# Attention states per head, in two float16 halves spread over 96 partitions, in place of a float32 product of four heads

## The chip, the cores and the metric

One Trainium2 chip, one core. The metric is the device time of one execution in microseconds (us). The work is spread over TensorE (PE, with its weight loads PEld), VectorE (DVE), ScalarE (ACT), GpSimd (POOL) and SyncE (SP), whose instruction stream issues nearly all DMAs into one hardware queue. Each engine runs its own instructions strictly in order.

## What is computed

Eight batches of 512 rows by 512 pass through a feed-forward block, an attention block and a second feed-forward block, each added to its input. The part that the change touches is the attention: 16 heads of 32, a row of 512 tokens in four chunks of 128, and a state S of 32x32 per head carried from chunk to chunk:

```python
def step(S, qkv_c):
    qi, ki, vi = qkv_c
    scores = jnp.einsum('bhtd,bhsd,hts->bhts', qi, ki, mask)
    intra = jnp.einsum('bhts,bhsd->bhtd', scores, vi)
    cross = jnp.einsum('bhtd,ht,bhde->bhte', qi, lam_t, S)
    o = scale * (intra + cross)
    kv = jnp.einsum('bhtd,ht,bhte->bhde', ki, lam_rev, vi)
    return (lam_T * S + kv, o)
```

lam_t is exp(-s t) for token t of a chunk, lam_rev exp(-s (128 - t)), lam_T exp(-128 s). A feed-forward block is silu(x W1) * (x W3), a Hadamard transform folded into W2, and a product with it.

## The kernel before

**Passes and slots.** There are 16 feed-forward passes (two per batch, in the list ORDER). A pass has 16 steps j; step j is `gate` (12 matmuls of 512 columns into g_bank), `lin` (12 into l_bank) and `down` of step j-1 (12 into the four d_banks). After each of the three lies a *slot*: pieces of the norms and of the attention are put there by hand, in `attention_slots`, so that PE has them between two blocks of 12. The attention of batch b starts at slot 1+78b; it has four groups of four heads, 12 slots apart, 32 groups in all. Every engine walks the same list STEPS and issues what it has of each step, so this list sets the order on every engine. The slots of a group, counted from its own slot `at`, are: q and k at -6 to -3, `kturn` (decayed keys, kdec) at -2, the first score at 0, and then what the diff shows.

**The last steps of a pass.** At step 0 of a pass comes `down` of the pass before, then `resid` 0 and 1 (DVE reads d_bank, L1146); `resid` 2 and 3 follow the gate of step 1. After `resid` 3 the queue of SP has the store of the 1 MB result (x_dram, L596, or out_dram, L593), and, when the pass was a first feed-forward, the load of the next input (xin, 1 MB, L599). `down` of step 0 waits for all four `resid`.

**A group.** `score` c is four matmuls (keys ks, queries qs, both spread over 96 partitions as three blocks of 32: high, high and low halves of float16 numbers) into a_bank 0. DVE multiplies by the mask (L1304), ACT rounds to float16 (L940), DVE takes the rest (L1309), and `pv` c uses both halves. `kv` makes three products kdec x values of 128x128 in a_bank 1, of which the 32x32 blocks on the diagonal are the heads' own; DVE multiplies by a block mask, diag (L1314). `state` makes two steps S = lam_T S + kv on 128x128 (L1326). `pv` c adds in a_bank 1, for chunks after the first, the float32 product of qdec and state (L1514) and per head two float16 products (L1519 with 64 columns, L1521 with 32). Two chunks share the bank, and one DVE reduction (L1332) takes both. qdec is the queries times lam_t, made on POOL (L715).

**Spreading.** q and k are stored to parts_dram and loaded again as three blocks each (L644, L650), since a DMA alone moves data between partitions here.

Of the kernel before, what the change touches and what calls it, by code (L numbers as in the profile page):

```python
# [7 lines left out]
ALU = mybir.AluOpType  # L8
# [16 lines left out]
SCORE_SCALE = 2.0 ** -20  # L25


def macaron_kernel(nc, x, qkv_w, qkv_norm_w, proj_w, proj_norm_w, norm_w, s, w1, w2, w3, out):
# [24 lines left out]
    with ctx:  # L53
# [3 lines left out]
        def sem(name):  # L57
# [21 lines left out]
        sizes = dict(x1=TT * D, hid=2 * D, gate=D, hfull=D, x2=TT * D, yt=KT * T, qs=HG * T // 2, ks=HG * T // 2, qdec=T,  # L79
                     kdec=(TT - 1) * P, flow=T, sc=2 * HG * P, state=(TT - 1) * P)  # L80
# [11 lines left out]
        gate, hfull, qdec, flow = at["gate"], at["hfull"], at["qdec"], at["flow"]  # L92
# [31 lines left out]
        state = at["state"].rearrange("p (c e) -> p c e", c=TT - 1)  # L124
        first = sizes["x1"] + sizes["hid"] + sizes["gate"] + sizes["hfull"]
# [28 lines left out]
        lam_rev = sb("lam_rev", [P, HEADS])  # L154
        lam_T = sb("lam_T", [P, GROUPS])
        diag = sb("diag", [P, P])
# [52 lines left out]
        q_hi, q_lo, q_dec = sem("q_hi"), sem("q_lo"), sem("q_dec")  # L209
# [10 lines left out]
        state_done = sem("state_done")  # L220
# [61 lines left out]
        def attention_slots():  # L282
# [11 lines left out]
            for b in range(B):  # L294
# [5 lines left out]
                for g in range(GROUPS):  # L300
# [118 lines left out]
        def bank_use(step, arg):  # L419
            if step in ("turn", "v"):  # L420
                return arg[1] % 2, 2
            if step == "proj":
                return arg[1] % 2, 1
            if step == "pv":
                return (1, 1) if arg[2] % 2 == 0 else None
            return {"q": (0, 1), "k": (0, 1), "score": (0, 1), "kv": (1, 1)}.get(step)
# [4 lines left out]
        for step, arg in STEPS:  # L431
# [6 lines left out]
            elif step == "pv":  # L438
                USES[step, arg] = USES["pv", arg[:2] + (arg[2] - 1,)]
# [44 lines left out]
        def _(sp):  # L484
# [34 lines left out]
            for step, arg in STEPS:  # L519
# [109 lines left out]
                elif step == "klow":  # L629
# [8 lines left out]
                    if ag:  # L638

                        b, fill = filled("score", ((ag - 1) // GROUPS, (ag - 1) % GROUPS, TT - 1))  # L640
                        sp.wait_ge(a_ready[b], fill)
# [4 lines left out]
                elif step == "kspread":  # L646
                    ag = arg[0] * GROUPS + arg[1]
                    sp.wait_ge(k_stored, 16 * (ag + 1))
                    for i, part in enumerate((0, 0, 1)):
                        sp.dma_start(ks[HD * i:HD * (i + 1)],  # L650
                                     parts_dram[ag % 2, 1, :, part].rearrange("(h p) t -> p h t", h=HG)).then_inc(k_moved, 16)
                elif step == "split":
# [26 lines left out]
        def _(pool):  # L679
# [17 lines left out]
            for step, arg in STEPS:  # L697
# [8 lines left out]
                elif step == "q":  # L706
                    b, g = arg
                    if g:

                        bank_pv, fill = filled("pv", (b, g - 1, TT - 1))  # L710
                        pool.wait_ge(a_ready[bank_pv], fill)

                    bank_q, _ = filled(step, arg)
                    pool.wait_ge(a_free[bank_q], copied(step, arg, bank_q) + 1)
                    nc.gpsimd.tensor_tensor(qdec.rearrange("p (c t) -> p c t", c=TT), qT[:].rearrange("p (c t) -> p c t", c=TT),  # L715
                                            lam_t[:, g:g + 1, :].to_broadcast([P, TT, P]), ALU.mult).then_inc(q_dec, 1)
# [29 lines left out]
                elif step == "decay":  # L746
# [6 lines left out]
                    nc.gpsimd.iota(junk[:, P:2 * P], [[1, P]], base=0, channel_multiplier=0,  # L753
# [9 lines left out]
        def _(act):  # L763
# [14 lines left out]
            for step, arg in STEPS:  # L778
# [43 lines left out]
                elif step == "decay":  # L822
# [7 lines left out]
                    for g in range(GROUPS):  # L830
                        nc.scalar.activation(lam_t[:, g, :], junk[:, P:2 * P], ACT.Exp, scale=s_col[:, g:g + 1])

                    nc.scalar.activation(decay_bound[:], decay_bound[:], ACT.Exp, scale=float(P)).then_inc(decay_top, 1)
                    nc.scalar.activation(lam_rev[:], s_row[:], ACT.Exp, scale=tiny[:, 0:1])
# [57 lines left out]
                elif step == "q":  # L892
# [3 lines left out]
                    if ag:  # L896

                        act.wait_ge(q_lo, ag)
                        act.wait_ge(q_dec, ag)
# [31 lines left out]
                elif step == "kturn":  # L931

                    act.wait_ge(kd_f32, arg[0] * GROUPS + arg[1] + 1)
                    nc.scalar.copy(kdec[:, 0, :], kT[:, 0:(TT - 1) * P]).then_inc(kd_hi, 1)
                elif step == "score":
# [7 lines left out]
        def _(dve):  # L943
# [34 lines left out]

            link(nc.vector.memset(diag[:], 0.0))
            for h in range(HG):  # L980
                nc.vector.memset(diag[HD * h:HD * (h + 1), HD * h:HD * (h + 1)], SCORE_SCALE)

            for step, arg in STEPS:
# [88 lines left out]
                elif step == "fit":  # L1072
# [6 lines left out]
                    nc.vector.tensor_scalar(lam_rev[:], lam_rev[:], decay_bound[:], None, ALU.mult)  # L1079
# [110 lines left out]
                elif step == "ostat":  # L1190
                    a, t = arg

                    b, _ = filled("pv", (a, GROUPS - 1, 2))
                    dve.wait_ge(a_free[b], copied("pv", (a, GROUPS - 1, 2), b) + 1)
# [86 lines left out]
                elif step == "kturn":  # L1281
# [5 lines left out]
                    for c in range(TT - 1):  # L1287
                        decayed = kT[:, P * c:P * (c + 1)].rearrange("p (h d) -> p h d", h=HG)
                        ins = nc.vector.tensor_tensor(decayed, decayed, lam_rev[:, HG * arg[1]:HG * (arg[1] + 1)].rearrange("p (h a) -> p h a", a=1)
# [20 lines left out]
                elif step == "kv":  # L1310
# [17 lines left out]
                elif step == "pv" and arg[2] % 2:  # L1328
# [3 lines left out]
                    nc.vector.tensor_reduce(x2[:, c - 1:c + 1, P * g:P * (g + 1)],  # L1332
# [223 lines left out]
```

## Time and profile before

| | |
|---|---|
| median of 3 runs | 2354.49 us (2353.8 to 2356.52) |
| the profiled execution | 2355.63 us, span 2353.9 us |
| PE busy | 2336.4 us (99%) |
| DVE / ACT / POOL busy | 1232.0 / 692.4 / 149.8 us |
| mean granted PE clock | 0.999 of full speed |
| moved by DMA | 196.83 MB, 84 GB/s |

The span is the stretch between the first and the last instruction in the trace; the own time of the profiled execution has 1.73 us more around it. A busy share counts an engine as busy while any of its instructions is in flight; matmuls overlap, so the start times of PE's pieces say more than their durations.

### The profile page before, as it was taken

The page shows a single profiled execution, that of the slowest core. Times are in us where ns is not written, and L with a number is a line of the kernel's source. Part 1 is how long each engine was busy: PE and PEld are TensorE (multiplying, and loading weights), DVE is VectorE, ACT ScalarE, POOL GpSimd, SP SyncE. Part 2 cuts the span into 40 slices and gives each one's busy share as a digit, 9 for nine tenths or more (in the row PEclk, how much of TensorE's full clock was granted, in tenths as well). Part 3 has the DMA queues.
Part 4 walks back from the last instruction along what each step waited for, and adds up shares of the span by engine and source line. Part 5 has one row for each costly group of instructions (what it writes and reads, how often), then busy time and mean ns, then how long its engine had stood idle before and what let it go on. Part 6 is the DMA issues. An engine that isn't in the chain of part 4 may idle for free.

```text
span 2353.9 us, 31017 instructions
## 1 busy us (share of the span) xinstructions
PE 2336.4 (99%) x12407; PEld 1120.7 (48%) x12407; DVE 1232.0 (52%) x2211; ACT 692.4 (29%) x1164; POOL 149.8 (6%) x126
## 2 busy tenths in 40 slices
PE   8999999999999999999999999999999999999999
PEld 4444444444544454445444444445444544544444
DVE  6577555654565446546554465544664455445212
ACT  6645233222222222223223222222232213221211
POOL 0190000000000000000000000000000000000000
PEclk9999999999999999999999999999999999999999
DMA  8856622331243212422042223421432224131200
GB/s 218 229 152 175 157 86 64 89 86 50 68 77 107 72 28 82 103 75 64 28 138 51 54 81 90 99 54 28 121 68 85 50 54 99 31 87 36 65 25 19
DMA packets 299457, 196.83 MB, mean 84 GB/s; under 512 B 231600, under 2 KB 256176, under 8 KB 295472
## 3 DMA queue, kind: packets, MB, share of 16 engines
q1 hardware_dynamic: 299024, 194.31, 31.6%
q8 instruction: 98, 1.61, 0.3%
q10 hardware_dynamic: 288, 0.52, 0.1%
q14 instruction: 47, 0.39, 0.1%
HBM read 84.68 MB, written 54.53 MB: 59 GB/s over the span
## 4 chain that ended last, share of the span: by engine, by line
PE 94%; DVE 3%; issue 1%; ACT 1%; DMA 1%; SPq 0%; POOL 0%; DVEq 0%; ACTq 0%; POOLq 0%
PE d_bank L1437 27%; PE l_bank L1417 27%; PE g_bank L1417 26%; PE a_bank L1472 5%; PE a_bank L1532 2%; PE a_bank L1455 2%; PE a_bank L1483 1%; PE a_bank L1514 1%; PE a_bank L1519 1%; PE a_bank L1497 1%; DVE work L1146 1%; DVE work L1126 0%; DMA w1t<-kT 0%; PE a_bank L1521 0%; PE d_bank L1391 0%
## 5 line engine op out<-in xcount | busy, mean ns | idle before, releaser
L1437 PE MATMUL d_bank<-w2t,work 128*128 128x512 f16 x2940 | 671.9, 379 | 0.0
L1437 PEld LDWEIGHTS d_bank<-w2t,work 128*128 128x128 f16 x2940 | 284.7, 98 | 332.4 <-DVE work L1146 0.6
L1126 DVE SCALAR_TENSOR_TENSOR work<-l_bank,l_scale,work 128x512 f32<-128x512 f32 x256 | 191.8, 749 | 468.4 <-PE l_bank L1417 468.4
L1417 PE MATMUL g_bank<-xt,w1t 128*128 128x512 f16 x1536 | 354.1, 380 | 3.6 <-DMA w1t<-kT 3.6
L1417 PE MATMUL l_bank<-xt,w3t 128*128 128x512 f16 x1536 | 352.4, 379 | 0.0
L857 ACT ACTIVATE work<-g_bank,g_scale 128x512 f32<-128x512 f32 x256 | 175.4, 685 | 490.1 <-PE g_bank L1417 488.2
L876 ACT CAST work<-work 128x512 f16<-128x512 f32 x232 | 143.3, 618 | 562.0 <-DVE work L1126 561.1
L1417 PE MATMUL l_bank<-work,w3t 128*128 128x512 f16 x1344 | 308.4, 379 | 0.2 <-DVE work L1126 0.2
L1417 PE MATMUL g_bank<-work,w1t 128*128 128x512 f16 x1344 | 308.3, 379 | 0.0
L1417 PEld LDWEIGHTS g_bank<-xt,w1t 128*128 128x128 f16 x1536 | 148.3, 98 | 177.9 <-DMA w1t<-kT 4.6
L1417 PEld LDWEIGHTS l_bank<-xt,w3t 128*128 128x128 f16 x1536 | 148.1, 98 | 173.0 <-issue 0.2
L1417 PEld LDWEIGHTS l_bank<-work,w3t 128*128 128x128 f16 x1344 | 129.6, 98 | 152.6 <-DVE work L1126 0.7
L1417 PEld LDWEIGHTS g_bank<-work,w1t 128*128 128x128 f16 x1344 | 129.7, 98 | 152.1
L1133 DVE TENSOR_TENSOR work<-work 128x512 f16<-128x512 f32 x232 | 160.3, 691 | 60.2 <-ACT work L876 59.5
L1309 DVE TENSOR_TENSOR work<-work 128x512 f16<-128x512 f32 x128 | 88.6, 692 | 88.1 <-ACT work L940 88.1
L884 ACT CAST cent<-cent 128x512 f16<-128x512 f32 x124 | 76.5, 617 | 173.8 <-DVE cent L1240 60.3
L1472 PE MATMUL a_bank<-zt,wqkv 128*128 128x512 f16 x512 | 121.0, 379 | 0.0
L940 ACT CAST work<-work 128x512 f16<-128x512 f32 x128 | 79.0, 618 | 126.8 <-DVE work L1304 126.8
L715 POOL TENSOR_TENSOR work<-qT,lam_t 128x512 f32<-128x512 f32 x32 | 40.7, 1271 | 1071.8 <-ACT qT L900 1071.8
L1260 DVE TENSOR_TENSOR cent<-cent 128x512 f16<-128x512 f32 x124 | 85.3, 688 | 35.1 <-ACT cent L884 32.8
L705 POOL TENSOR_TENSOR rstd<-veps,half 128x4 f32<-128x4 f32 x32 | 37.0, 1156 | 891.6 <-DVE veps L1188 546.9
L1304 DVE SCALAR_TENSOR_TENSOR work<-a_bank,mask 128x512 f32<-128x512 f32 x128 | 87.3, 682 | 2.1
(227 smaller groups left out, 1791.1 us busy)
## 6 DMA issues: line engine op xcount, KB each, us to landing
work<-parts_dram SPq DMA_DIRECT2D x192, 128.0 KB, 2.7
x_dram<-work SPq DMA_DIRECT2D x16, 1024.0 KB, 4.2
work<-x_dram SPq DMA_DIRECT2D x11, 1024.0 KB, 6.6
parts_dram<-q_parts SPq DMA_DIRECT2D x32, 256.0 KB, 2.0
parts_dram<-k_parts SPq DMA_DIRECT2D x32, 256.0 KB, 2.2
norm_dram<-cent SPq DMA_DIRECT2D x32, 256.0 KB, 2.0
w2t<-in_L_ffn_W_dram SPq DMA_DIRECT2D x30, 256.0 KB, 3.2
xin<-in_L_attn_x_dram SPq DMA_DIRECT2D x7, 1024.0 KB, 8.4
```

Of the source, the lines that this page charges most:

```text
L857: nc.scalar.activation(gate, g_bank[:], ACT.Silu, scale=g_scale[:, j:j + 1]).then_inc(gate_ready, 1)
L876: nc.scalar.copy(parts[:, 0, :], hfull).then_inc(hi_ready, 1)
L884: nc.scalar.copy(halves[:, t % 2, 0, :], centred).then_inc(ln_hi, 1)
L940: nc.scalar.copy(sc[:, c % 2, 0], flow.rearrange("p (h t) -> p h t", h=HG)).then_inc(sc_hi, 1)
L1126: nc.vector.scalar_tensor_tensor(out=hfull, in0=l_bank[:], scalar=l_scale[:, j:j + 1], in1=gate, op0=ALU.mult, op1=ALU.mult).then_inc(hful ...
L1133: nc.vector.tensor_tensor(parts[:, 1, :], hfull, parts[:, 0, :], ALU.subtract).then_inc(lo_ready, 1)
L1260: nc.vector.tensor_tensor(halves[:, t % 2, 1, :], centred, halves[:, t % 2, 0, :], ALU.subtract).then_inc(ln_lo, 1)
L1304: nc.vector.scalar_tensor_tensor(out=masked, in0=a_bank[b][:].rearrange("p (h t) -> p h t", h=HG), scalar=SCORE_SCALE, in1=mask[:, HG * g: ...
L1309: nc.vector.tensor_tensor(sc[:, c % 2, 1], masked, sc[:, c % 2, 0], ALU.subtract).then_inc(sc_lo, 1)
L1417: ins = nc.tensor.matmul(dst[:], wt[:, wp, k, P * j:P * (j + 1)], src[:, xp, k, :], start=(k == 0 and wp == xp), stop=(k == KT - 1 and wp ...
L1437: ins = nc.tensor.matmul(d_bank[t][:], parts[:, hp, P * t:P * (t + 1)], w2t[:, j, wp, :], start=(j == 0 and hp == wp), stop=(j == HT - 1 a ...
L1472: ins = nc.tensor.matmul(a_bank[b][:], wqkv[:, k, col:col + P], zt[:, part, k, :], start=(k == 0 and part == 0), stop=(k == KT - 1 and par ...
```

## The change

The states are kept per head as 32 columns instead of 128 (DVE copies the diagonal blocks of `kv`, four instructions of 32 partitions), rounded into two float16 halves by ACT and DVE, stored to state_dram, and loaded as three blocks of 32 partitions into `states` (high, high, low). `pv` multiplies per head the *undecayed* queries qs (high, low, high) of the scores with them, on 96 partitions and 32 columns, into a region of its own of a_bank 1, and DVE multiplies this region by the decay lam_out when it takes the result, then adds the two others. Each chunk now takes a_bank 1 for itself. qdec and its POOL product are gone, as are lam_t and diag. Scales that are powers of two (lift, lower) keep the halves in range. `kv` and `state` come one slot earlier, `pv` 1 to 3 one slot later.

```diff
-                    add(slots, at, [("score", (b, g, 0))])
-                    add(slots, at + 1, [("kv", (b, g)), ("score", (b, g, 1)), ("state", (b, g))])
-                    for c in range(TT):
-                        add(slots, at + 2 + c, [("pv", (b, g, c))] + ([("score", (b, g, c + 2))] if c < TT - 2 else []))
+                    add(slots, at, [("kv", (b, g)), ("state", (b, g)), ("score", (b, g, 0))])
+                    add(slots, at + 1, [("score", (b, g, 1)), ("statestore", (b, g))])
+                    add(slots, at + 2, [("pv", (b, g, 0)), ("score", (b, g, 2)), ("statespread", (b, g))])
+                    add(slots, at + 4, [("pv", (b, g, 1)), ("score", (b, g, 3))])
+                    add(slots, at + 5, [("pv", (b, g, 2))])
+                    add(slots, at + 6, [("pv", (b, g, 3))])
...
+                elif step == "statestore":
+                    ag = arg[0] * GROUPS + arg[1]
+                    sp.wait_ge(state_lo, ag + 1)
+                    if ag >= 2:
+
+                        sp.wait_ge(state_moved, 16 * BLOCKS * (ag - 1))
+                    sp.dma_start(state_dram[ag % 2], state_parts).then_inc(state_stored, 16)
+                elif step == "statespread":
+                    ag = arg[0] * GROUPS + arg[1]
+                    sp.wait_ge(state_stored, 16 * (ag + 1))
...
+                    for i, part in enumerate((0, 0, 1)):
+                        sp.dma_start(states[HD * i:HD * (i + 1)],
+                                     state_dram[ag % 2, :, part].rearrange("(h p) c e -> p h c e", h=HG)).then_inc(state_moved, 16)
...
-                    nc.gpsimd.tensor_tensor(qdec.rearrange("p (c t) -> p c t", c=TT), qT[:].rearrange("p (c t) -> p c t", c=TT),
-                                            lam_t[:, g:g + 1, :].to_broadcast([P, TT, P]), ALU.mult).then_inc(q_dec, 1)
...
+                elif step == "state":
+                    ag = arg[0] * GROUPS + arg[1]
+                    act.wait_ge(state_done, (TT - 2) * (ag + 1))
...
+                    nc.scalar.copy(state_parts[:, 0], state).then_inc(state_hi, 1)
...
-            link(nc.vector.memset(diag[:], 0.0))
-            for h in range(HG):
-                nc.vector.memset(diag[HD * h:HD * (h + 1), HD * h:HD * (h + 1)], SCORE_SCALE)
...
+                    nc.vector.tensor_scalar(lam_out[:, 0], lam_out[:, 0], SCORE_SCALE / STATE_SCALE, None, ALU.mult)
+
+                    nc.vector.tensor_scalar(lower_col[:], lam_T[:], 1.0, None, ALU.max)
+                    link(nc.vector.tensor_scalar(lift[:], lift[:], 1.0, None, ALU.max))
...
+                    link(power(lower[:], lift[:], True))
...
+                    for c in range(1, TT - 1):
+                        nc.vector.tensor_tensor(lam_rev[:, c], lam_rev[:, c - 1], lower[:], ALU.mult)
+                        link(nc.vector.tensor_tensor(lam_out[:, c], lam_out[:, c - 1], lift[:], ALU.mult))
...
-                    nc.vector.tensor_tensor(state, a_bank[b][:, 0:(TT - 1) * P].rearrange("p (c e) -> p c e", c=TT - 1),
-                                            diag[:].rearrange("p (a e) -> p a e", a=1).to_broadcast([P, TT - 1, P]),
-                                            ALU.mult).then_inc(a_free[b], 1)
+                    products = a_bank[b][:, 0:(TT - 1) * P].rearrange("p (c h e) -> p c h e", c=TT - 1, h=HG)
+                    for h in range(HG):
+
+                        rows_h = slice(HD * h, HD * (h + 1))
+                        ins = nc.vector.tensor_scalar(state[rows_h], products[rows_h, :, h], STATE_SCALE, None, ALU.mult)
+                    ins.then_inc(a_free[b], 1)
...
+                    dve.wait_ge(state_hi, ag + 1)
+                    nc.vector.tensor_tensor(state_parts[:, 1], state, state_parts[:, 0], ALU.subtract).then_inc(state_lo, 1)
...
+                        nc.vector.tensor_tensor(o.rearrange("p (h e) -> p h e", h=HG), turns[:, 0].rearrange("p (h e) -> p h e", h=HG),
+                                                lam_out[:, c - 1, HG * g:HG * (g + 1)].rearrange("p (h a) -> p h a", a=1)
+                                                .to_broadcast([P, HG, HD]), ALU.mult).then_inc(o_sum, 1)
+                        dve.wait_ge(o_sum, done + 1)
+                        nc.vector.tensor_tensor(o, turns[:, 1], o, ALU.add).then_inc(o_sum, 1)
+                        dve.wait_ge(o_sum, done + 2)
+                        nc.vector.tensor_tensor(o, turns[:, 2], o, ALU.add).then_inc(a_free[b], 1)
...
+                    if c == 1:
+                        pe.wait_ge(state_moved, 16 * BLOCKS * (a * GROUPS + (g + 1)))
...
-                        nc.tensor.matmul(halves_o[:, 0, :], qdec[:, P * c:P * (c + 1)], state[:, c - 1, :],
-                                         start=(c == 2), stop=False, skip_group_check=True)
...
+                            ins = nc.tensor.matmul(turns[:, 0, cols], qs[0:BLOCKS * HD, h, P * c:P * (c + 1)],
+                                                   states[0:BLOCKS * HD, h, c - 1, :], start=False, stop=True, skip_group_check=True)
```

SP's queue in group 3 of batch 2, which starts with step 0 of a pass. Before the change (L644 and L650 load the queries and keys, L596 stores the result of the pass that ends, L599 loads the next input, L663 is the next norm):

```order
L644 DMA work<-parts_dram 32x4x512 x3
L650 DMA work<-parts_dram 32x4x512 x3
L596 DMA x_dram<-work 128x2048
L599 DMA xin<-in_L_attn_x_dram 128x4x512
L663 DMA_TRANSPOSE zt<-cent 128x8x128
```

and with the change, at the same place (L604 and L607 are the store and the load, L666 stores the states, L675 spreads them):

```order
L652 DMA work<-parts_dram 32x4x512 x3
L658 DMA work<-parts_dram 32x4x512 x3
L666 DMA state_dram<-work 128x192
L604 DMA x_dram<-work 128x2048
L607 DMA xin<-in_L_attn_x_dram 128x4x512
L675 DMA work<-state_dram 32x4x96 x3
L688 DMA_TRANSPOSE zt<-cent 128x8x128
```

The two transfers of 1 MB now stand between the store of the states and their spreading. They stand so in groups 0 of batch 0, 3 of batch 2 and 2 of batch 4; in group 1 of batch 6 it is the 1 MB store of an output alone.

DVE in the same group, before (L1126 is `lin`, L1304 and L1309 a score, L1133 `low`, L1146 `resid`, L1314 `kv`, L1326 `state`):

```order
L1126 SCALAR_TENSOR_TENSOR work<-l_bank,l_scale,work 128x512
L1304 SCALAR_TENSOR_TENSOR work<-a_bank,mask 128x512
L1309 TENSOR_TENSOR work<-work 128x512
L1133 TENSOR_TENSOR work<-work 128x512
L1146 SCALAR_TENSOR_TENSOR work<-d_bank,ffn_unscale,xin 128x512 x2
L1314 TENSOR_TENSOR work<-a_bank,diag 128x384
L1304 SCALAR_TENSOR_TENSOR work<-a_bank,mask 128x512
L1309 TENSOR_TENSOR work<-work 128x512
L1326 SCALAR_TENSOR_TENSOR work<-work,lam_T 128x128 x2
L1146 SCALAR_TENSOR_TENSOR work<-d_bank,ffn_unscale,xin 128x512 x2
```

and with the change (L1156, L1334, L1339, L1163, L1176 are the same steps under new line numbers; L1348 copies the diagonal blocks, L1359 is the recurrence, L1363 the low halves):

```order
L1156 SCALAR_TENSOR_TENSOR work<-l_bank,l_scale,work 128x512
L1348 TENSOR_SCALAR work<-a_bank 32x96 x4
L1359 SCALAR_TENSOR_TENSOR work<-work,lam_T 128x32 x2
L1363 TENSOR_TENSOR work<-work 128x96
L1334 SCALAR_TENSOR_TENSOR work<-a_bank,mask 128x512
L1339 TENSOR_TENSOR work<-work 128x512
L1163 TENSOR_TENSOR work<-work 128x512
L1176 SCALAR_TENSOR_TENSOR work<-d_bank,ffn_unscale,xin 128x512 x2
L1334 SCALAR_TENSOR_TENSOR work<-a_bank,mask 128x512
L1339 TENSOR_TENSOR work<-work 128x512
L1176 SCALAR_TENSOR_TENSOR work<-d_bank,ffn_unscale,xin 128x512 x2
```

All the work on the states now stands ahead of the first score and of the four `resid`.

## Rows read from the trace of the kernel before

**Rows 1.** The page's chain that ended last: share of the span by engine.

```profile
PE 94%; DVE 3%; issue 1%; ACT 1%; DMA 1%; SPq 0%; POOL 0%; DVEq 0%; ACTq 0%; POOLq 0%
```

**Rows 2.** Timeline of PE, one `pv` and a score: start us, us, engine, line.

```profile
556.46 0.38 PE L1514 MATMUL a_bank<-work 128*128 128x128 f32 x2
556.68 0.19 PE L1519 MATMUL a_bank<-work 128*128 128x64 f16 x1
...
556.90 0.38 PE L1483 MATMUL a_bank<-work 96*128 96x128 f16 x4
```

**Rows 3.** Groups by line and shape: busy us, mean ns, idle before.

```profile
L994 DVE TENSOR_SCALAR k_turned_parts<-k_turned_parts 128x4 f32<-128x4 f32 x7 | 1.2, 170 | 0.2
L934 ACT CAST work<-kT 128x384 f16<-128x384 f32 x32 | 16.3, 511 | 58.2 <-DVE kT L1289 58.2
```

**Rows 4.** Timeline of DVE in an ordinary group (group 0 of batch 2).

```profile
545.47 0.56 DVE L1294 TENSOR_TENSOR work<-kT,work 128x384 f16<-128x384 f32 x1 [0.58 <-ACT work L934]
547.49 0.75 DVE L1126 SCALAR_TENSOR_TENSOR work<-l_bank,l_scale,work 128x512 f32<-128x512 f32 x1 [1.46 <-PE l_bank L1417]
...
553.26 0.73 DVE L1326 SCALAR_TENSOR_TENSOR work<-work,lam_T 128x128 f32<-128x128 f32 x2
```

**Rows 5.** DMA issues of the page: KB each, median us to landing.

```profile
work<-parts_dram SPq DMA_DIRECT2D x192, 128.0 KB, 2.7
parts_dram<-q_parts SPq DMA_DIRECT2D x32, 256.0 KB, 2.0
xin<-in_L_attn_x_dram SPq DMA_DIRECT2D x7, 1024.0 KB, 8.4
zt<-cent SPq DMA_TRANSPOSE x68, 3.4
```

**Rows 6.** Timeline of DVE in group 3 of batch 2: second score, `resid` 2 and 3.

```profile
906.34 0.68 DVE L1304 SCALAR_TENSOR_TENSOR work<-a_bank,mask 128x512 f32<-128x512 f32 x1
...
908.96 1.40 DVE L1146 SCALAR_TENSOR_TENSOR work<-d_bank,ffn_unscale,xin 128x512 f32<-128x512 f32 x2
```

**Rows 7.** Timeline of PE in the same group.

```profile
901.12 0.39 PE L1483 MATMUL a_bank<-work 96*128 96x128 f16 x4
901.34 2.75 PE L1437 MATMUL d_bank<-w2t,work 128*128 128x512 f16 x12
903.93 0.67 PE L1497 MATMUL a_bank<-work 128*128 128x128 f16 x9
904.44 0.39 PE L1483 MATMUL a_bank<-work 96*128 96x128 f16 x4
...
911.02 0.40 PE L1483 MATMUL a_bank<-work 96*128 96x128 f16 x4
```

**Rows 8.** Timeline of SP's issues in the same group.

```profile
910.39 0.34 SPq L596 DMA_DIRECT2D x_dram<-work  x1
910.78 0.43 SPq L599 DMA_DIRECT2D xin<-in_L_attn_x_dram  x1
```

**Rows 9.** DMA issues of 460.6 to 461.8 us: KB each, us to landing.

```profile
xin<-in_L_attn_x_dram SPq DMA_DIRECT2D x1, 1024.0 KB, 8.3
zt<-cent SPq DMA_TRANSPOSE x1, 8.9
```

**Rows 10.** A stretch: length, busy PE, PEld, DVE, ACT, POOL, granted clock, DMA, GB/s.

```profile
38.00:40.00 2.00, 2.00 (x6) 0.76 (x5) 0.16 (x1) 0.00 (x0) 0.00 (x0) 0.50 1.22 287
```

**Rows 11.** Timeline of PE: a block of 12 after a wait, and a score after one.

```profile
36.02 4.45 PE L1417 MATMUL g_bank<-xt,w1t 128*128 128x512 f16 x12 [2.83 <-DMA w1t<-kT]
...
308.50 0.40 PE L1483 MATMUL a_bank<-work 96*128 96x128 f16 x4 [0.75 <-DVE work L1304]
```

**Rows 12.** Timeline of DVE: the block mask at the start, and the four `resid` of pass 0.

```profile
5.42 0.47 DVE L981 MEMSET diag<- 32x32 f32 x4
...
248.93 2.72 DVE L1146 SCALAR_TENSOR_TENSOR work<-d_bank,ffn_unscale,xin 128x512 f32<-128x512 f32 x4
```

**Rows 13.** The chain in order of time: start us, us, what (`down` of passes 0 and 1).

```profile
208.60 72.52 PE d_bank L1437 x336
```

More of the change, by code:

```diff
@@ L25 @@
 SCORE_SCALE = 2.0 ** -20
+STATE_SCALE = 2.0 ** -23
 def macaron_kernel(nc, x, qkv_w, qkv_norm_w, proj_w, proj_norm_w, norm_w, s, w1, w2, w3, out):
@@ L77, in macaron_kernel @@
         junk = qT
-        sizes = dict(x1=TT * D, hid=2 * D, gate=D, hfull=D, x2=TT * D, yt=KT * T, qs=HG * T // 2, ks=HG * T // 2, qdec=T,
-                     kdec=(TT - 1) * P, flow=T, sc=2 * HG * P, state=(TT - 1) * P)
+        sizes = dict(x1=TT * D, hid=2 * D, gate=D, hfull=D, x2=TT * D, yt=KT * T, qs=HG * T // 2, ks=HG * T // 2,
+                     kdec=(TT - 1) * P, flow=T, sc=2 * HG * P, state=(TT - 1) * HD, state_parts=(TT - 1) * HD,
+                     states=HG * (TT - 1) * HD // 2)
         early_use = sizes["x1"] + sizes["hid"] + sizes["gate"] + sizes["hfull"] + KT * H + 2 * T
@@ L124, in macaron_kernel @@
         state = at["state"].rearrange("p (c e) -> p c e", c=TT - 1)
+        state_parts = at["state_parts"].bitcast(F16).rearrange("p (a c e) -> p a c e", a=2, c=TT - 1)
+        states = at["states"].bitcast(F16).rearrange("p (h c e) -> p h c e", h=HG, c=TT - 1)
+        state_dram = nc.dram_tensor("state_dram", [2, P, 2, TT - 1, HD], F16, kind="Internal").ap()
         first = sizes["x1"] + sizes["hid"] + sizes["gate"] + sizes["hfull"]
@@ L424, in bank_use @@
             if step == "pv":
-                return (1, 1) if arg[2] % 2 == 0 else None
+                return 1, 1
             return {"q": (0, 1), "k": (0, 1), "score": (0, 1), "kv": (1, 1)}.get(step)
@@ L638, in _ @@
                     if ag:
-                        b, fill = filled("score", ((ag - 1) // GROUPS, (ag - 1) % GROUPS, TT - 1))
+                        b, fill = filled("pv", ((ag - 1) // GROUPS, (ag - 1) % GROUPS, TT - 1))
                         sp.wait_ge(a_ready[b], fill)
@@ L829, in _ @@
                     ins.then_inc(decay_exp, 1)
-                    for g in range(GROUPS):
-                        nc.scalar.activation(lam_t[:, g, :], junk[:, P:2 * P], ACT.Exp, scale=s_col[:, g:g + 1])
                     nc.scalar.activation(decay_bound[:], decay_bound[:], ACT.Exp, scale=float(P)).then_inc(decay_top, 1)
-                    nc.scalar.activation(lam_rev[:], s_row[:], ACT.Exp, scale=tiny[:, 0:1])
+                    nc.scalar.activation(lam_rev[:, 0], s_row[:], ACT.Exp, scale=tiny[:, 0:1])
+                    nc.scalar.activation(lam_out[:, 0], s_row[:], ACT.Exp, scale=tiny[:, 11:12])
+                    nc.scalar.activation(lift[:], s_row[:], ACT.Exp, scale=float(P))
                     nc.scalar.activation(lam_T[:], s_col[:], ACT.Exp, scale=float(P)).then_inc(act_const, 1)
@@ L1327, in _ @@
                                                        in1=state[:, c, :], op0=ALU.mult, op1=ALU.add).then_inc(state_done, 1)
-                elif step == "pv" and arg[2] % 2:
+                    dve.wait_ge(state_hi, ag + 1)
+                    nc.vector.tensor_tensor(state_parts[:, 1], state, state_parts[:, 0], ALU.subtract).then_inc(state_lo, 1)
+                elif step == "pv":
                     a, g, c = arg
@@ L1331, in _ @@
                     dve.wait_ge(a_ready[b], fill)
-                    nc.vector.tensor_reduce(x2[:, c - 1:c + 1, P * g:P * (g + 1)],
-                                            a_bank[b][:].rearrange("p (c a e) -> p c e a", c=2, a=2), AX.X, ALU.add
-                                            ).then_inc(a_free[b], 1)
+                    turns = a_bank[b][:].rearrange("p (r e) -> p r e", r=4)
+                    o = x2[:, c, P * g:P * (g + 1)]
+                    if c == 0:
+                        nc.vector.tensor_reduce(o, turns[:, 1:3].rearrange("p a e -> p e a"), AX.X, ALU.add).then_inc(a_free[b], 1)
+                    else:
+                        done = 2 * ((a * GROUPS + g) * (TT - 1) + c - 1)
+                        nc.vector.tensor_tensor(o.rearrange("p (h e) -> p h e", h=HG), turns[:, 0].rearrange("p (h e) -> p h e", h=HG),
[5 more added lines that the diff above has]
+                        nc.vector.tensor_tensor(o, turns[:, 2], o, ALU.add).then_inc(a_free[b], 1)
                 elif step == "proj":
```

66 lines of the change are left out of this document (32 added, 34 removed).

## The prediction

> **What bounds the kernel now.** I read the page's chain first: 94% of the span is PE, 1% DMA [rows 1], so a microsecond taken from PE is a microsecond of the result, and so is every wait put before PE. Then PE's timeline through one group, for what each small product really costs; then DVE and SP through an ordinary group and through a group that meets the end of a pass, for what reaches PE late. POOL's product, which the change removes, ends nothing on this chain.
>
> **PE's own work.** Durations overlap; start times count. The float32 product begins at 556.46 and the next matmul at 556.68: 0.22 us. The eight small ones take 556.68 to 556.90, 27.5 ns each, the 32-column ones no less than the 64-column ones [rows 2]. The new cross product is four of 32 columns, 4 x 27.5 ns = 0.11 us. Gain 0.11 us per chunk, for the 3 chunks of each of 32 groups that have a cross term, 96 in all: **-10.6 us**. Bounds: if a 32-column matmul next to another took half, -15.5; if each took 55 ns, as the four 128-column scores take, 0. I take the row of its own shape.
>
> The Trainium skill (TensorE: Matmul & The Clock Gate, Wait — 56ns, not 53.3ns?) says that start-to-start never falls below about 25 ns however few the columns. The trace's 27.5 ns agrees; by the page's figure the gain would be 11.5 us.
>
> **An ordinary group.** Times from the score at 547.29, which now gives its place to `kv`. Its keys kdec end at 546.03 [rows 4], so the earlier `kv` finds them. `kv` takes 0.5, 903.93 to 904.44 [rows 7]. DVE is free of `lin` at 548.2 [rows 4]. Then come four copies of 32x96: a DVE operation of 4 columns takes 0.17, one step on 128 columns 0.73/2 = 0.36 [rows 3, 4]; I take 0.18 each, 0.7; two state steps on 32 columns at 0.25, 0.5; ACT's rounding 0.3 (384 columns take 0.51 [rows 3]); the low half 0.2. The halves are ready at about 549.9. The store lands in 2.0, the three loads are issued 0.46 apart (one issue takes 0.43 [rows 8]) and each lands in 2.7 [rows 5]: about 555.6. PE asks for them in `pv` 1, behind four blocks of 2.59 (901.34 to 903.93 [rows 7]), `kv`, two scores, `pv` 0 and a third: 559.0. They are hidden with 3.4 us over. DVE's longer `pv` (three operations of 128 columns in place of half a reduction, 0.9 us) has a block of 2.59 before the bank is wanted. So the ordinary groups, 28 of 32, cost nothing. If the margin were gone, each us of lateness would cost 28.
>
> **The four groups at the end of a pass.** In group 3 of batch 2 the state work, 0.7 + 0.5 + 0.3 + 0.2 = 1.7, now stands before the first score; of it 0.46 stood there already for `kv` and 0.65 for the steps before `resid` 2. Three things follow.
>
> First, the second score leaves its bank 1.7 - 0.46 = 1.2 later than 906.34 + 0.61, at 908.2; PE, with nothing else late, wants it at 907.46: a wait of 0.8. Now the group has 0.3, before the fourth score (904.44 + 0.22 + 2 x 2.59 + 2 x 0.44 = 910.72, begun at 911.02 [rows 7]), which the longer wait replaces. **+0.5** in three such groups and in group 3 of batch 4, where a norm loads DVE in the same way: +2.0. In group 0 of batch 0 the second score follows the first at once; it waits 0.75 already [rows 11], and 1.2 of the 1.7 reaches it: +1.2.
>
> Second, and larger, SP. `resid` 3 ends at 910.36 [rows 6]; SP issues the store at 910.39 and the load of xin at 910.78 [rows 8]. Here `resid` 3 moves by 1.7 - 0.46 - 0.65 = 0.6, the load to 911.4, and only behind it can SP issue the spreading, 911.85 to 912.8. A transfer issued behind such a load lands with it: the transpose issued at 460.72, 0.5 after an xin load that took 8.3, took 8.9 itself [rows 9] where the median is 3.4 [rows 5]. So the states land about 0.6 after xin: 911.4 + 8.4 (median [rows 5]) + 0.6 = 920.4. PE arrives at `pv` 1 at 901.12 + 0.72 (kv, score) + 2.59 + 0.22 + 2.59 + 0.22 + 0.8 (wait) + 0.22 + 2 x 2.59 = 913.65. Wait: **+6.7**, in three groups: +20.2. In group 1 of batch 6 only the store of an output stands ahead: issued 911.85 to 912.8 by the same count and 2.7 to land, 915.5, 1.9 late without any queue; with the store 2.2.
>
> Third, the clock. After a wait of 2.83 us PE's granted clock falls from its full level, 2.4 GHz, to 0.50, 1.2 GHz [rows 10], and a block of 12 takes 4.45 instead of 2.75 [rows 11]: 1.7 lost. A wait of 7 us should do the same: 3 x 1.7 = **+5.1**, 0 if it doesn't, up to twice that if the low level lasts longer.
>
> The Trainium skill (DMA: Bandwidth & Descriptors, Queues, rings and completion order) says that on each DMA engine descriptors are consumed in ring order, all DMAs issued from SP sharing one ring on each. It speaks against this change; the trace agrees (8.9 beside 3.4). By that rule alone, with the load's 8.4 and nothing after it, the three waits would be 6.1 each, 1.8 less in all.
>
> **Constants and start.** `fit` gains 13 small DVE operations before the four `resid` of pass 0. Five are waited for, 0.17 each; the rest take between 0.08 pipelined and 0.17 [rows 3]: 1.5 to 2.2, taken 1.65. `resid` starts at 248.93 [rows 12], then 250.6, first one done at 251.25. PE's 192 matmuls of pass 0 end at 208.60 + 192 x 0.2155 = 249.95 [rows 13]: +1.3. The block mask of DVE's start goes (0.47 and its clearing, 0.7 in all) [rows 12]; the first weights' transfers hide most of it, since PE waits for one at 36.02 [rows 11]: -0.3, between 0 and -0.7.
>
> **Sum.** -10.6 + 2.0 + 1.2 + 20.2 + 2.2 + 5.1 + 1.3 - 0.3 = +21.1. Against the profiled execution, 2355.63, that is 2376.7; it stands 1.1 above the median of the runs shown, so 2375.6 on that.
>
> **Rivals.**
> (a) *The spreading isn't held by the transfers ahead of it.* It lands 2.7 after its last issue, 915.5 in place of 920.4, with no clock lost: four waits of 1.9. -10.6 + 2.0 + 1.2 + 7.6 + 1.3 - 0.3 = +1.2, 2355.7. For it: the transfer is small, 24 KB a load. Against: rows 9. Chance 0.12.
> (b) *Faster: the spreading is hidden everywhere.* Its place is `pv` 1 of the four groups; it decides if the states land by 913.65 there, 1.8 after the first issue. Then the waits of 1.9 go too: -6.4, 2348.1. Against: no load of this kind has a median below 2.7. Chance 0.07.
> (c) *The states are late in all groups:* 96 columns make rows of 192 bytes where the queries have 1024, but as many of them; if three such loads took 4.4 longer than I reckon, the margin of 3.4 would be exceeded by 1 and 28 groups would add 28: 2404. Chance 0.08.
> (d) *The new products don't save:* 55 ns each, gain 0, rest as forecast: 2386.2. Chance 0.04.
> The likeliest keeps 0.69; its own range is 2366 to 2387 (waits of 5.5 to 8.5, clock 0 to 10).
>
> **How the numbers follow.** 0.2%, 4.7 us, is about what a measurement of this kernel tells from no change: 2349.8 to 2359.2 is "same". Faster 0.08 (b, a little of a), same 0.11 (a), slower 0.81. The range from 2355 to 2388 takes in (a), (d) and the likeliest, and leaves out (b) and (c), 0.15, and a tail.
>
> **What the profile after would show.** Right: PE waiting for a DMA state_dram to work, some 7 us, three times, near 318, 914 and 1360, and 2 us once near 1815; the granted clock 0.5 after each of the three; `pv` 1 to 3 in 0.33 us; SP's spreading issued 0.5 behind xin and landing in 8 to 9 where elsewhere it takes under 3; PE waiting about 1.3 for `resid` near 250. Wrong, if the spreading lands in 3 us behind xin (a or b); if PE waits for state_dram in ordinary groups (c); if the twelve matmuls of a `pv` take more than 0.4 (d); if PE waits for DVE's three `pv` operations, which I count as hidden.

## The result and the profile after

The changed kernel takes 2395.04 us (median of 4 runs, 2393.99 to 2395.81) where the kernel before, now with a fourth run, takes 2354.15 (2353.8 to 2356.52): ratio 1.017, 95% interval 1.0158 to 1.0182. The forecast was 2375.6 with 2355 to 2388: slower, as said, but by 40.9 us and not by 21, and outside the range. The profiled execution's span is 2392.9 us, 39.0 more than before.

The page's chain by engine, which answers to [rows 1], shows where PE's share went: 94% before, now

```profile
PE 83%; DVE 7%; issue 3%; POOL 3%; DMA 2%; ACT 1%; SPq 1%; DVEq 0%; POOLq 0%; ACTq 0%
```

The view of waits on PE names them (us in total, times, longest). The first row is the spread states, forecast as 22.4 us. The second is the scores' bank; before it was 1.3 us, and the forecast added 3.2:

```profile
PE a_bank L1558 <- DMA work<-state_dram: 19.2, 4, 6.3
PE a_bank L1530 <- DVE work L1334: 18.4, 35, 3.0
PE l_bank L1464 <- DVE work L1156: 4.1, 4, 3.2
...
PE d_bank L1484 <- DVE work L1176: 1.8, 1, 1.8
```

**Where the 39 us lie.** Laid side by side, the starts of PE's blocks of both traces drift apart like this:

| stretch | forecast | measured |
|---|---|---|
| start, up to the last chunk of pass 1's first products (before's 208 us) | -0.3 | -3.2 |
| `fit` | +1.3 | +1.9 |
| group 0 of batch 0 | +9.3 | +8.5 |
| group 3 of batch 2 | +8.6 | +8.8 |
| group 2 of batch 4 | +8.6 | +9.4 |
| group 1 of batch 6 | +2.4 | +5.6 |
| group 3 of batch 4, group 3 of batch 1 | +0.2, -0.3 | +1.6, +1.2 |
| the 26 other groups | 26 x -0.33 = -8.6 | 26 x +0.20 = +5.2 |
| sum | +21.2 | +39.0 |

**An ordinary group.** PE's timeline in group 0 of batch 2 of the changed kernel (start us, us):

```profile
798.51 0.67 PE L1544 MATMUL a_bank<-work 128*128 128x128 f16 x9
799.01 0.39 PE L1530 MATMUL a_bank<-work 96*128 96x128 f16 x4
799.24 2.75 PE L1484 MATMUL d_bank<-w2t,work 128*128 128x512 f16 x12
802.37 0.40 PE L1530 MATMUL a_bank<-work 96*128 96x128 f16 x4 [0.38 <-DVE work L1334]
```

The second score is due at 799.24 + 2.59 = 801.83 and starts at 802.37, 0.54 late, for the bank that the first score still holds. DVE's timeline at the same place says why:

```profile
799.38 1.04 DVE L1348 TENSOR_SCALAR work<-a_bank 32x96 f32<-32x96 f32 x4
800.45 0.54 DVE L1359 SCALAR_TENSOR_TENSOR work<-work,lam_T 128x32 f32<-128x32 f32 x2
801.33 0.26 DVE L1363 TENSOR_TENSOR work<-work 128x96 f16<-128x96 f32 x1 [0.34 <-ACT work L954]
801.62 0.69 DVE L1334 SCALAR_TENSOR_TENSOR work<-a_bank,mask 128x512 f32<-128x512 f32 x1
```

The state work takes 799.38 to 801.62, 2.24 us where the forecast had 1.7, and only behind it does DVE take the first score out of the bank.

**Group 3 of batch 2.** SP's issues, to be held beside [rows 8]: the spreading, L675, is issued from 922.85, behind the store L604 and the load L607, though the states were stored at 914.61.

```profile
914.61 0.35 SPq L666 DMA_DIRECT2D state_dram<-work  x1
921.93 0.34 SPq L604 DMA_DIRECT2D x_dram<-work  x1
922.31 0.44 SPq L607 DMA_DIRECT2D xin<-in_L_attn_x_dram  x1
922.85 2.56 SPq L675 DMA_DIRECT2D work<-state_dram  x3
```

The DMA issues of 922 to 926.5 us (KB each, median us to landing), which answer to [rows 9]:

```profile
xin<-in_L_attn_x_dram SPq DMA_DIRECT2D x1, 1024.0 KB, 8.2
work<-state_dram SPq DMA_DIRECT2D x3, 24.0 KB, 6.3
```

PE there, and the stretches around its wait (length, busy PE, PEld, DVE, ACT, POOL, granted clock, DMA, GB/s):

```profile
919.26 0.40 PE L1530 MATMUL a_bank<-work 96*128 96x128 f16 x4 [0.70 <-DVE work L1334]
...
931.18 0.21 PE L1558 MATMUL a_bank<-work 128*128 128x64 f16 x1 [6.34 <-DMA work<-state_dram]
...
931.99 4.02 PE L1464 MATMUL g_bank<-xt,w1t 128*128 128x512 f16 x12
936.17 1.02 PE L1464 MATMUL l_bank<-xt,w3t 128*128 128x512 f16 x4
```

```profile
930.00:935.00 5.00, 3.81 (x25) 1.93 (x26) 2.16 (x5) 0.62 (x1) 0.00 (x0) 0.54 0.00 1
935.00:940.00 5.00, 5.00 (x46) 2.63 (x45) 1.88 (x6) 0.94 (x2) 0.00 (x0) 1.00 0.01 3
```

The wait is 6.34. From the block behind it to the next it is 936.17 - 931.99 = 4.18, of which the `pv` between the two takes 0.32; the block itself has 3.86 instead of 2.59. The granted clock of that stretch is 0.54: 1.2 GHz for most of it. The three other waits for states are 3.95, 5.95 and 2.98.

**Group 0 of batch 0.** Here the second score follows the first with no block between them, and PE loses time at the scores already:

```profile
309.45 0.40 PE L1530 MATMUL a_bank<-work 96*128 96x128 f16 x4 [3.02 <-DVE work L1334]
309.69 4.44 PE L1464 MATMUL g_bank<-xt,w1t 128*128 128x512 f16 x12
```

The wait is 3.02 where before had 0.75 [rows 11], and the block behind it runs at the low clock too: 4.28 from its start to the next matmul of another line instead of 2.59.

### The profile page after: what moved, and what is told of

Read it like the earlier page. It is cut to its first block, busy times and chain, and to the rows that moved or that the text cites. A ratio compares the mean times of both kernels' runs of the same rounds, so it can differ in the third digit from the quotient of the medians.

```text
span 2392.9 us, 31988 instructions
## 1 busy us (share of the span) xinstructions
PE 2337.2 (98%) x12599; PEld 1100.5 (46%) x12599; DVE 1282.0 (54%) x2603; ACT 699.9 (29%) x1194; POOL 109.0 (5%) x94
## 4 chain that ended last, share of the span: by engine, by line
PE 83%; DVE 7%; issue 3%; POOL 3%; DMA 2%; ACT 1%; SPq 1%; DVEq 0%; POOLq 0%; ACTq 0%
PE g_bank L1464 25%; PE l_bank L1464 25%; PE d_bank L1484 22%; PE a_bank L1519 5%; PE a_bank L1502 2%; PE a_bank L1574 2%; DVE work L1348 1%; POOL work L751 1%; DVE work L1156 1%; DVE work L1334 1%; PE a_bank L1530 1%; POOL work L750 1%; DMA work<-state_dram 1%; PE a_bank L1558 1%; DVE work L1359 1%
## 5 line engine op out<-in xcount | busy, mean ns | idle before, releaser
L1156 DVE SCALAR_TENSOR_TENSOR work<-l_bank,l_scale,work 128x512 f32<-128x512 f32 x256 | 191.6, 748 | 443.8 <-PE l_bank L1464 443.7
L1163 DVE TENSOR_TENSOR work<-work 128x512 f16<-128x512 f32 x232 | 160.4, 691 | 61.8 <-ACT work L890 61.1
L1339 DVE TENSOR_TENSOR work<-work 128x512 f16<-128x512 f32 x128 | 88.6, 692 | 88.0 <-ACT work L960 88.0
L1334 DVE SCALAR_TENSOR_TENSOR work<-a_bank,mask 128x512 f32<-128x512 f32 x128 | 87.6, 684 | 1.0
L1300 DVE TENSOR_TENSOR k_parts<-kT,k_parts 128x512 f16<-128x512 f32 x32 | 22.2, 693 | 104.7 <-ACT k_parts L932 104.7
```

Of the source, the lines that this page charges most:

```text
L1156: nc.vector.scalar_tensor_tensor(out=hfull, in0=l_bank[:], scalar=l_scale[:, j:j + 1], in1=gate, op0=ALU.mult, op1=ALU.mult).then_inc(hful ...
L1163: nc.vector.tensor_tensor(parts[:, 1, :], hfull, parts[:, 0, :], ALU.subtract).then_inc(lo_ready, 1)
L1334: nc.vector.scalar_tensor_tensor(out=masked, in0=a_bank[b][:].rearrange("p (h t) -> p h t", h=HG), scalar=SCORE_SCALE, in1=mask[:, HG * g: ...
L1339: nc.vector.tensor_tensor(sc[:, c % 2, 1], masked, sc[:, c % 2, 0], ALU.subtract).then_inc(sc_lo, 1)
```

## The experiments

Theory A: two separate causes. DVE's state work stands ahead of the first score's evacuation (0.54 us in nearly every group), and the spreading is issued behind 1 MB transfers in four groups (the long waits and the low clock). Against it: the first wait comes with the new operations whatever their order, or the states land late wherever SP issues them. Gains between medians are taken through the ratios to the kernel before, which ran 15 times beside each set of kernels: 2355.31 beside the two single edits, the kernel with both and the one with only the load moved, 2353.18 beside the other four.

### The first score ahead of the states

```diff
-                    add(slots, at, [("kv", (b, g)), ("state", (b, g)), ("score", (b, g, 0))])
+                    add(slots, at, [("score", (b, g, 0)), ("kv", (b, g)), ("state", (b, g))])
```

> The changed kernel with one line of its plan altered: in the group's first slot the first score stands ahead of kv and state again, so that VectorE evacuates the first score (L1334) before the four copies and the two steps of the state. Theory A (in every ordinary group the second score's matmul waits for L1334, which stands behind some 3.3 us of copies, steps and the low half, .53 us more from start to start in 28 groups): those waits go, 2395.0 - 28 x .53 = 2380, and the three .70 us waits at the first score's successor in groups 11, 18 and 25 go too, so 2376 to 2382. Rival B (the state work only changes places and the second score then waits as long for its own turn, or the wait sits in the longer product): no change, 2393 to 2396. Rival C (the state is stored later, and the second output's matmul waits for the spread states in every group): slower, above 2397, with waits at L1558 put down to state_dram in ordinary groups.

Measured 2387.87 (2382.64 to 2388.91), ratio 1.0133 (1.0119 to 1.0146), some 9 us less than the change; the profiled execution was the fastest, span 2380.9, 12.0 less. PE's waits in its trace:

```profile
PE a_bank L1558 <- DMA work<-state_dram: 21.4, 4, 6.3
PE a_bank L1530 <- DVE work L1334: 8.1, 8, 1.6
```

Of 35 waits 8 are left. In each ordinary group the blocks behind the second score start 0.55 us earlier, and 0.10 of that is lost again at the third score: 0.45 net. In the groups of the long waits the gain is given back. In group 0 of batch 0 the states land when they did, so PE, 2.2 us earlier, waits 6.11 for them instead of 3.95 (hence 21.4 for 19.2 in all). In the three others the wait moves to the third score, 1.26 us in group 3 of batch 2, where the second and third scores had 0.38 and 0.70. The mechanism is shown by the trace; the median fell short of the 2376 to 2382 expected. The three runs that were only timed stand 5 to 6 us above the profiled one, at a clock of 0.993 and 0.994 beside its 0.994; where they lose it isn't in a trace.

### The state work shortened, in the change's order

```diff
-                    for h in range(HG):
-
-                        rows_h = slice(HD * h, HD * (h + 1))
-                        ins = nc.vector.tensor_scalar(state[rows_h], products[rows_h, :, h], STATE_SCALE, None, ALU.mult)
+                    ins = nc.vector.tensor_scalar(state, products[:, :, 0], STATE_SCALE, None, ALU.mult)
```

> The changed kernel with its order kept, but with one copy of 128 x 96 from the bank (head 0's columns for all rows) in place of the four per head; it leaves out the gathering of heads 1 to 3, so its states are not the reference's. VectorE's work ahead of the first score's evacuation is shorter by 3 x 0.25 = 0.75 us. Theory A (the second score waits .53 us in each ordinary group because the state work, 2.24 us, is that much too long for one slot): the wait is gone, as in the kernel with the first score ahead, and the ordinary groups give back 28 x .53, at the profile 12 to 15 us: 2380 to 2385. Rival (the order alone costs, whatever the length, for instance through the hand-over from PE to VectorE and ScalarE): under 4 us are given back, 2391 to 2396.

The kernel leaves out the columns of heads 1 to 3, so it is a test of time alone. Measured 2373.96 (2373.19 to 2375.39), ratio 1.0084 (1.007 to 1.0098): 20 us less than the change. DVE and PE in the same group of it:

```profile
796.86 0.25 DVE L1345 TENSOR_SCALAR work<-a_bank 128x96 f32<-128x96 f32 x1
797.15 0.54 DVE L1356 SCALAR_TENSOR_TENSOR work<-work,lam_T 128x32 f32<-128x32 f32 x2
798.02 0.26 DVE L1360 TENSOR_TENSOR work<-work 128x96 f16<-128x96 f32 x1 [0.34 <-ACT work L954]
798.20 0.69 DVE L1334 SCALAR_TENSOR_TENSOR work<-a_bank,mask 128x512 f32<-128x512 f32 x1
```

```profile
796.50 0.39 PE L1527 MATMUL a_bank<-work 96*128 96x128 f16 x4
799.32 0.39 PE L1527 MATMUL a_bank<-work 96*128 96x128 f16 x4
```

State work of 1.34 us leaves no wait in an ordinary group: the second score starts 2.82 us behind the first, 3.36 in the change. It is 0.55 us per ordinary group again, here with nothing lost at the third score. The time is lower than the 2380 to 2385 expected: the groups that meet `resid` don't give the gain back as in the kernel above, and in group 1 of batch 6 the wait for the states was 2.12 us and PE kept its clock (1.7 us). The order alone doesn't cost; the length does, in this order.

### The change's order in the kernel before

```diff
-                    add(slots, at, [("score", (b, g, 0))])
-                    add(slots, at + 1, [("kv", (b, g)), ("score", (b, g, 1)), ("state", (b, g))])
+                    add(slots, at, [("kv", (b, g)), ("state", (b, g)), ("score", (b, g, 0))])
+                    add(slots, at + 1, [("score", (b, g, 1))])
```

> The kernel before with kv and state moved ahead of the first score, as the changed kernel has them, and nothing else. Theory A (the order costs only what the state work exceeds the slot by): here this work is .56 + .73 = 1.3 us where the changed kernel has 2.24 us, so about .4 us inside the slot; no wait in ordinary groups, and 2354 to 2358 in all (a few tenths in groups that meet the residual). Rival (the order costs by itself): 28 x .5 more, 2366 to 2370.

Measured 2355.55 (2353.53 to 2357.59), ratio 1.0005 (0.9996 to 1.0014). Its DVE in group 0 of batch 2:

```profile
545.85 0.55 DVE L1314 TENSOR_TENSOR work<-a_bank,diag 128x384 f32<-128x384 f32 x1
546.43 0.74 DVE L1326 SCALAR_TENSOR_TENSOR work<-work,lam_T 128x128 f32<-128x128 f32 x2
547.09 0.68 DVE L1304 SCALAR_TENSOR_TENSOR work<-a_bank,mask 128x512 f32<-128x512 f32 x1
```

545.85 to 547.09 is 1.24 us, and the ordinary groups stand where they stood, to 0.01 us; only those that meet `resid` or a norm lose 0.1 to 0.5 each. The most is in group 0 of batch 0, where the wait at the second score is 2.00 instead of 0.75. This and the kernel above close in on the cause from both sides.

### The spreading ahead of the 1 MB transfers

```diff
-                    add(slots, at + 1, [("score", (b, g, 1)), ("statestore", (b, g))])
-                    add(slots, at + 2, [("pv", (b, g, 0)), ("score", (b, g, 2)), ("statespread", (b, g))])
+                    add(slots, at + 1, [("score", (b, g, 1)), ("statestore", (b, g)), ("statespread", (b, g))])
+                    add(slots, at + 2, [("pv", (b, g, 0)), ("score", (b, g, 2))])
```

> The changed kernel with statespread one slot earlier, right behind statestore in the group's second slot, so that in the groups where SyncE writes the residual and loads the next batch's rows (1 MB each way) the three spread transfers are issued ahead of these. Theory A (the waits at L1558 for state_dram in groups 0, 11, 18 and 25, 3.95 + 6.34 + 5.95 + 2.98 = 19.2 us, come from the spread being issued behind those transfers, and the stretches at half clock behind them, some 8 to 10 us, come from these waits): 2395.0 - 19.2 - 9 = 2367, range 2364 to 2376. Rival B (the spread lands late whatever stands ahead of it, since the engines' rings are full with the weights and rows): 2390 to 2395. Rival C (SyncE now stands some 2 us at the store's landing in each of 32 groups, and the q, k or operand transfers behind it come late): slower than 2395, with new waits for k_turned, q_moved or k_moved on PE or VectorE.

Measured 2368.7 (2366.54 to 2370.23), ratio 1.0054 (1.004 to 1.0068): 27 us less than the change. In its trace no wait for state_dram is left on PE, while the other group of waits stays (18.5 us, 35 times), and SP's issues in group 3 of batch 2 read

```profile
911.59 0.35 SPq L666 DMA_DIRECT2D state_dram<-work  x1
913.16 1.25 SPq L675 DMA_DIRECT2D work<-state_dram  x3
918.90 0.34 SPq L604 DMA_DIRECT2D x_dram<-work  x1
919.28 0.44 SPq L607 DMA_DIRECT2D xin<-in_L_attn_x_dram  x1
```

The three loads land in 1.8 us (median of that stretch) instead of 6.3. PE's blocks come earlier by 4.4, 6.8, 6.4 and 3.1 us at the four places, and by 1.2, 1.3, 2.3 and 1.7 more over the next block, which no longer runs at the low clock: 27.2 us in all. PE shows no new wait for anything that stands behind SP's wait for the store.

### Only the load behind the spreading

```diff
-                        if done.batch < B - 1:
+                        if pending and done.batch < B - 1:
+                            held.append(done.batch + 1)
+                        elif done.batch < B - 1:
...
+                    pending.append(ag)
...
+                    pending.clear()
+                    while held:
+                        sp.dma_start(xin[:], x_tiles[bass.ds(held.pop() * TT, TT)].rearrange("t p d -> p t d")
+                                     ).then_inc(x_loaded, 16)
```

> The changed kernel; where SyncE writes x1 between statestore and statespread of a group, the load of the next batch's rows into xin (1 MB) is issued right behind the spread instead of ahead of it; the write of 1 MB stays ahead. Theory A1 (the spread's packets queue behind the load's packets, whose landing takes 8.2 us): the waits at L1558 fall by most of their 6 us where the load stood ahead, some 12 of 19 us over the four groups, and with them half of the low-clock stretches: 2378 to 2386. Rival A2 (the write to DRAM ahead of the spread, or the late turn of SyncE itself behind the residual's semaphore, is what makes it late): 2391 to 2395. With the other run (spread ahead of both) it tells the load's share from the rest.

Measured 2379.59 (2377.98 to 2380.65), ratio 1.0101 (1.0088 to 1.0115). PE's waits, and the DMA issues of 914 to 924 us:

```profile
PE a_bank L1538 <- DVE work L1342: 18.5, 35, 3.0
PE a_bank L1566 <- DMA work<-state_dram: 7.2, 3, 2.8
```

```profile
x_dram<-work SPq DMA_DIRECT2D x1, 1024.0 KB, 4.2
xin<-in_L_attn_x_dram SPq DMA_DIRECT2D x1, 1024.0 KB, 7.1
work<-state_dram SPq DMA_DIRECT2D x3, 24.0 KB, 3.6
```

Of 19.2 us the load ahead made 12.0; the late turn of SP and the 1 MB store make the other 7.2, and no run separates these two. The loads of 24 KB land in 6.3 us behind store and load, in 3.6 behind the store, in 1.8 behind neither. The Trainium skill (DMA: Bandwidth & Descriptors, Queues, rings and completion order) says that each DMA engine consumes descriptors in ring order, and that all of SP's DMAs use one ring on each; these three landings agree with it.

### Both edits, and then the third score a slot later

> Both edits together: first score ahead of kv and state, and statespread right behind statestore. If the two causes are separate, as theory A has it, the gains add: 2395.0 - 17 - 28 = 2350, range 2347 to 2362, which would be no slower than the kernel before (2354.2). Rival: the state is ready about 1 us later with the first score ahead of it, SyncE waits longer for it in the second slot, and the sum of the two gains is not reached: 2362 to 2380.

Both edits together: 2353.61 (2352.51 to 2356.68, 11 runs), ratio 0.9995 (0.9986 to 1.0003), 41 us less than the change where the edits alone gave 9 and 27. The gains add, with some left over: in group 0 of batch 0 the time at the scores is no longer lost again at the states. The change stands level with the kernel before. What is left on PE is 8.3 us for L1334, 8 times, most of it where DVE is behind with `resid` and the third score, one slot behind the second, follows it too soon.

```diff
-                    add(slots, at + 2, [("pv", (b, g, 0)), ("score", (b, g, 2))])
+                    add(slots, at + 2, [("pv", (b, g, 0))])
+                    add(slots, at + 3, [("score", (b, g, 2))])
```

> The kernel with both edits (first score ahead, spread early; 2353.6) with the third score one slot later, at the group's fourth slot, which is empty there. Its profile has 8 waits of PE at the scores' matmuls for L1334, 8.3 us in all, in groups that meet VectorE's residual work. Theory: the third score no longer waits for the second's evacuation; 5 to 8 us go: 2346 to 2349. Rival: PE meets VectorE's backlog one instruction later (the residual's work is what is late, not the score), and the waits move to the second output or to L1156: 2351 to 2355.

Measured 2344.35 (2341.84 to 2345.67), ratio 0.9956 (0.9944 to 0.9969), a little better than the 2346 to 2349 expected. Its waits:

```profile
PE l_bank L1465 <- DVE work L1157: 3.7, 3, 3.2
...
PE a_bank L1559 <- DVE work L1382: 2.1, 2, 1.1
...
PE d_bank L1485 <- DVE work L1177: 1.6, 1, 1.6
PE a_bank L1531 <- DVE work L1335: 1.0, 2, 0.8
```

Of 8.3 us for the scores 1.0 is left, 0.8 has moved to the outputs (L1382). Each ordinary group is 0.10 shorter besides: in the kernel with both edits the second score left its bank at 793.86 + 0.69 = 794.55 in group 0 of batch 2, and the third began at 794.61, just behind it.

### The constants moved out of `fit`

```diff
+                if j == 6:
+                    steps += [("powers", 0)]
...
+                elif step == "powers":
```

The block of DVE from lam_out's scaling to the last lam_out goes under this step, unchanged.

> The same kernel as the one with the third score later, and with the new constants (the powers for the queries and states, some 20 instructions of VectorE on 128 x 16) taken out of the step fit and put some 20 us later, behind the seventh chunk of the second matrix. Theory: PE's wait at L1484 for the residual (1.2 us there, 1.75 in the changed kernel) goes back to what it was, 1.2 to 1.9 us less than that kernel. Rival: the wait has another cause (the row scaling of nw_row and of decay_bound, which stays): no difference, within 0.5 us.

Measured 2342.12 (2341.31 to 2343.75), ratio 0.9949 (0.9937 to 0.9962). The wait at L1177 is gone and PE is 1.60 us earlier from there on. The two intervals overlap, so it is the traces and not the medians that show this gain. This kernel has the lowest median of all, 52 us below the change as it was made.

## Why the forecast was wrong, step by step

**The step that failed: "So the ordinary groups, 28 of 32, cost nothing."** It followed the states to `pv` 1 (hidden, as the trace shows: no ordinary group waits for state_dram) and DVE's longer `pv` (hidden too), but not the first score, which was moved behind the state work. The paragraph on the pass ends did reckon such a wait, for the bank of the second score. Applied here with the forecast's own numbers it is tight: DVE is free 0.9 after `kv` starts, 1.7 of state work, 0.61 to take the score (the row it starts from has 0.68 [rows 6]): 3.2, and PE wants the bank after 0.5 + 0.22 + 2.59 = 3.3. A margin of 0.1 called for a rival with a chance of its own. With the measured 2.24 it is 0.87 + 2.24 + 0.69 = 3.8, half a microsecond late, in nearly every group. 26 groups at +0.20 instead of -0.33 are 13.8 of the 17.8 us by which the sum fell short.

**The term mis-sized: the state work, 1.7, measured 2.24.** The four copies take 1.07 (799.38 to 800.45) where 0.7 was put: 0.25 us each, not 0.18. The forecast had rows for 4 columns, 0.17, and for 128, 0.36, and put 96 columns almost at the lower one. Two thirds of the 0.54 missing is this term; the rest is in the steps, the rounding and the low half (1.17 for 1.0). With 1.34 or 1.24 us no ordinary group waits, as two experiments show.

**PE's products: right.** `pv` 1 now takes 810.82 to 811.14, 0.32 us, for 0.44 before [rows 2]: 0.12 for 0.11 forecast. It shows in the result once the waits are gone: each ordinary group of the last kernels is 0.36 shorter than before.

```profile
810.82 0.19 PE L1558 MATMUL a_bank<-work 128*128 128x64 f16 x1
810.84 0.18 PE L1560 MATMUL a_bank<-work 128*128 128x32 f16 x1
810.87 0.18 PE L1564 MATMUL a_bank<-work 96*128 96x32 f16 x1
...
811.14 0.38 PE L1530 MATMUL a_bank<-work 96*128 96x128 f16 x4
```

**The spreading behind the load: right in place, cause and size.** Forecast 3 x 6.7 + 2.2 = 22.4, measured 3.95 + 6.34 + 5.95 + 2.98 = 19.2. The first is shorter because PE had already lost 3.02 at the score before it and 1.7 by the clock. Rivals (a) and (b) are out; (c) and (d) too.

**Group 0 of batch 0: near the mark by luck.** The forecast subtracts from the 1.7 what stood ahead for `kv` already, and lets 1.2 reach the second score. But in before's order `kv` stands behind the first score, and no block lies between the two scores, so all of the state work reaches PE: with 1.24, 1.34 and 2.24 us of it the wait is 2.00, 2.09 and 3.02, that is 1.25, 1.34 and 2.27 more than before's 0.75. With the clock lost there this is 2.3 + 1.7 where 1.2 stood, and the wait for the states is 3.95 where 6.7 stood; so the group came to 8.5 for 9.3.

**The clock: right mechanism, too few places.** Three blocks at 1.7 each were forecast; the blocks behind the four waits for states lose 1.2, 1.3, 2.3 and 1.7 against 2.59, and the one behind the 3.02 at the score 1.7. The fourth, in group 1 of batch 6, has no term in the forecast, which put the wait there at 2.2 and not at 2.98; its 1.7 is about half of the 3.2 us missed in that group.

**Two more groups.** In group 3 of batch 4 PE waits 1.00 and 0.34 for DVE's new `pv` operations (L1381), which the forecast counted as hidden, and in group 3 of batch 1 1.34 for L1334: 2.7 us together.

**`fit`: right, +1.9 for 1.3.** The wait is 1.75, and moving the operations gives back 1.60.

**The start: -0.3 forecast, -3.2 seen, and the change isn't the cause.** The profiled execution of before had PE at the low clock at 36 us [rows 10, 11] and again at 190; that of the change had neither. But the kernel with the spreading moved has the same first 200 us as the change, and shows the block at the low clock:

```profile
34.83 4.45 PE L1464 MATMUL g_bank<-xt,w1t 128*128 128x512 f16 x12 [2.21 <-DMA w1t<-kT]
```

while the kernel before in the change's order, with before's own start, has none there and is 2.9 us earlier at 208 us. These stretches come and go from one execution to the next; before's 15 runs of a session spread from 2351.77 to 2358.7 at clocks of 0.997 to 1.0. So some 3 of the 39 us between the spans are luck against the forecast, and the medians' 40.9 is the better figure.

## What to carry to other kernels

When work is moved ahead of an instruction on an in-order engine, count what that instruction releases as well as what the moved work delivers, in the commonest case first: half a microsecond in each of 26 groups outweighed any of the four large waits. A margin of 0.1 us on estimates is no margin; compare it with the error of the estimate times the number of repeats. And give small transfers that PE will ask for a place in the issue queue ahead of large ones that nobody wants soon: that single place in the list was worth 27 us, and with the scores and constants moved too a change that lost 41 us is one that gains 11.

## What the runs showed of the hardware

A DVE copy of 96 columns takes 0.25 us on 32 partitions as on 128 (1.04 us for four of the one, 0.25 for one of the other): splitting by partitions multiplies the cost. The length of PE's wait alone doesn't decide the clock. In the kernel with the third score a slot later and in the last one, the same block follows the same wait, and ran at the low clock in one and at the full clock in the other:

```profile
187.72 4.04 PE L1465 MATMUL l_bank<-zt,w3t 128*128 128x512 f16 x12 [3.17 <-DVE work L1157]
188.46 2.76 PE L1467 MATMUL l_bank<-zt,w3t 128*128 128x512 f16 x12 [3.17 <-DVE work L1159]
```

Near 35 us a wait of 2.21 halved the clock, shorter than these. Behind each of the changed kernel's four waits for states, 2.98 to 6.34, and behind its 3.02 at a score, it was halved.
